# A place for each head pair's O in chunk 0, and all of Q of chunk 6 projected in chunk 5

## What is computed

```python
Q, K, V = split_heads(x @ WQ.T), split_heads(x @ WK.T), split_heads(x @ WV.T)   # 16 heads of 64
scores = where(causal, Q @ K.T / sqrt(64), NEG)
out = (softmax(scores) @ V) @ WO.T
x = layernorm(x + out)                                   # x: [16, 2048, 1024]
xn = x * rsqrt(mean(x * x) + 1e-6)
scale = 127.0 / max(abs(xn))                             # per row
xq = clip(round(xn * scale), -128, 127) / scale
x = layernorm(x + xq @ (w_int8 * weight_scale).T + bias)
```

## Time and profile before

| | us |
|---|---|
| runs of the kernel (median of 3) | 1003.89 (1002.97 to 1004.13) |
| the profiled execution | 1004.11 |
| its span on the slowest core (core 2) | 1002.6 |
| spans of the eight cores | 994.9 to 1002.6 |
| TensorE busy | 907.1 (90%) |
| ScalarE busy | 687.2 (69%) |
| VectorE busy | 519.0 (52%) |
| GpSimd busy | 227.4 (23%) |

### The profile page before, as it was taken

How to read it: one execution, slowest core, us unless ns; L and a number is a source line. 1 busy time by engine, 2 the same in 40 slices (tenths; PEclk the granted TensorE clock), 3 DMA queues, 4 the chain that set the end, 5 groups by cost and what they waited for, 6 DMA issues and landing times.

```text
span 1002.6 us, 22536 instructions; the slowest of 8 cores (994.9 to 1002.6 us)
## 1 busy us (share of the span) xinstructions
PE 907.1 (90%) x8267; PEld 409.9 (41%) x8416; DVE 519.0 (52%) x1263; ACT 687.2 (69%) x713; POOL 227.4 (23%) x290
## 2 busy tenths in 40 slices
PE   3894999999999989999999999999799999999863
PEld 1342444444444433434444444444344444444421
DVE  0110147744786327653127747762477523776675
ACT  0133666776877789999744566777577779999931
POOL 5021322231122121221223232232122211222101
PEclk9997999999999999999999999999899999999897
DMA  9999333250223141221154251144413210114212
GB/s 117 146 178 182 65 45 42 64 147 13 28 64 101 54 53 28 79 44 62 37 66 66 64 148 23 33 107 94 49 33 102 74 44 10 25 26 146 62 56 63
DMA packets 99289, 71.18 MB, mean 71 GB/s; under 512 B 70384, under 2 KB 88816, under 8 KB 99184
## 3 DMA queue, kind: packets, MB, share of 16 engines
q1 hardware_dynamic: 78368, 50.87, 20.5%
q0 software_dynamic: 20816, 18.88, 14.8%
HBM read 55.05 MB, written 16.78 MB: 72 GB/s over the span
## 4 chain that ended last, share of the span: by engine, by line
PE 77%; DMA 8%; ACT 6%; issue 3%; DVE 3%; POOL 1%; DVEq 0%; POOLq 0%; ACTq 0%; SPq 0%
PE ps L324 47%; PE ps L640 16%; PE ps L531 14%; ACT PT L559 5%; DMA WV<-wvt 4%; DMA QO<-OS 2%; DMA XT<-xt 1%; DVE OS L682 1%; DMA QT<-QB 1%; POOL PT L574 1%; ACT Q L844 1%; POOL WK L148 0%; POOL WQ L148 0%; DVE SM L678 0%; DVE Z L749 0%
## 5 line engine op out<-in xcount | busy, mean ns | idle before, releaser
L559 ACT ACTIVATE PT<-ps,SM 128x1024 bf16<-128x1024 f32 (+2 forms) x576 | 586.2, 1066 | 151.8 <-PE ps L531 149.8
L574 POOL TENSOR_TENSOR PT<-PT,MASK 128x256 bf16<-128x256 bf16 (+1 forms) x184 | 158.2, 867 | 506.0 <-ACT PT L559 505.8
L640 PE MATMUL ps<-VX,PT 128*128 128x65 bf16 x4352 | 235.1, 195 | 25.4 <-DVE OS L682 22.6
L640 PEld LDWEIGHTS ps<-VX,PT 128*128 128x128 bf16 x4352 | 179.2, 98 | 177.0 <-issue 141.9
L531 PE MATMUL ps<-QO,KT 64*128 64x512 bf16 (+1 forms) x1504 | 193.3, 325 | 10.9 <-ACT PT L559 10.2
L324 PE MATMUL ps<-XT,WK 128*128 128x512 bf16 x486 | 126.0, 386 | 23.8 <-DMA XT<-xt 22.4
L324 PE MATMUL ps<-W,QT 128*128 128x512 bf16 x477 | 128.6, 385 | 17.5 <-DMA QT<-QB 13.8
L324 PE MATMUL ps<-WO,QO 128*128 128x512 bf16 x474 | 127.0, 378 | 4.2 <-issue 1.7
L324 PE MATMUL ps<-XT,WQ 128*128 128x512 bf16 x485 | 124.6, 380 | 2.5 <-DMA WQ<-wqt 1.1
L324 PE MATMUL ps<-WV,XT 128*128 128x512 bf16 x489 | 124.1, 383 | 2.7 <-DMA WV<-wvt 1.4
L531 PEld LDWEIGHTS ps<-QO,KT 64*128 64x128 bf16 x1504 | 51.7, 94 | 182.2 <-issue 177.3
(11 more groups left out here) (50 smaller groups left out, 546.5 us busy)
## 6 DMA issues: line engine op xcount, KB each, us to landing
Z<-x SPq DMA_DIRECT2D x32, 512.0 KB, 4.4
y<-Z SPq DMA_DIRECT2D x32, 512.0 KB, 2.8
XT<-xt POOLq DMA_DIRECT2D x7, 1024.0 KB, 12.5
WK<-wkt POOLq DMA_DIRECT2D x4, 512.0 KB, 21.4
WQ<-wqt POOLq DMA_DIRECT2D x4, 512.0 KB, 24.6
WV<-wvt POOLq DMA_DIRECT2D x2, 1024.0 KB, 42.2
WO<-wot POOLq DMA_DIRECT2D x1, 2048.0 KB, 70.6
W<-w8t POOLq DMA_DIRECT2D x1, 2048.0 KB, 87.1
```

The costliest lines, as they stand in the source:

```text
L559: emit("s", lambda eng: eng.activation(dst, src, AF.Exp, bias=EB, scale=0.125).then_inc(sem["s"], 1))
L574: emit("g", lambda eng: eng.tensor_tensor(blk, blk, msk, ALU.mult).then_inc(sem["m"], 1))
L640: last = eng.matmul(ps[:, o_at + s_ * o_head + q * 65: o_at + s_ * o_head + q * 65 + 65], PT[:, pt0 + s_ * 512 + c0: pt0 + s_ * 512 + c0 + ...
```

## The change

There are two parts. In chunk 0 (su = 0) each head pair's normalized O has a place of its own: the pairs 0 and 1 in OS, the pairs 2 and 3 in O6, a bf16 view of the memory of Q16, and the pairs 4 to 7 in QT8. With that VectorE waits for no transpose in chunk 0, and each pair's transpose has a semaphore of its own. From chunk 1 on all is as before. And chunk 5 is treated like chunk 2: the four late projections of Q of chunk 6 stand at the end of the fillers of chunk 5 instead of at the head of those of chunk 6.

```diff
+        O6 = at("O6", [128, 1024], BF16, "q16")
...
+        for j in range(8):
             sem["ot%d" % j] = e(nc.semaphore("sem_ot%d" % j))
...
             wait("v", t_tok())
-            if i >= 2:
+            if su:
                 wait("v", tok_ot[(i - 2) // 8, (i - 2) % 8])
-            o0 = (i % 2) * 512
+            out, o_row, o0 = OS, 1024, (i % 2) * 512
+            if su == 0 and i >= 2:
+                out, o_row, o0 = ((O6, 1024, (i - 2) * 512) if i < 4 else
+                                  (QT8, 2048, (i - 4) * 512))
...
-                    ap(OS, o0, (1024, 128), (64, 2), (128, nq), (1, 64)),
+                    ap(out, o0, (o_row, 128), (64, 2), (128, nq), (1, 64)),
...
-            key = "ot%d" % (i % 2)
+            key = "ot%d" % (i % 2 if i >= 8 else i)
...
-                OS[:, o0:o0 + nq * 128]).then_inc(sem[key], 16))
+                out[:, o0:o0 + nq * 128]).then_inc(sem[key], 16))
...
-                if g == 2:
+                if g in (2, 5):
                     order, late = order + late, []
```

## The result

The change makes the kernel slower by 0.4%: the ratio of the time after to the time before is 1.0039 (95%: 1.0024 to 1.0054). Four runs of the changed kernel take 1005.97 to 1009.09 us, against a median of 1003.65 before; its other four (1052 to 1134 us) and one of the eight before are of a slower kind that some runs of either kernel fall into, and they are left out. The forecast was 1000.9 us, with a range to 1004.5: wrong in sign, and the result lies outside the range.

The account below looks back on a forecast made before the run. TensorE was taken to bound the kernel. Core 2: 1002.6-15.5+9.4+0.5+0.5 = 997.5 us; core 6: 1001.9-12.4+9.4+1.0+0.5 = 1000.4. With time outside the span, 1000.9 us was taken, nearer core 6; range 996.5 to 1004.5.

Parts of the forecast that it names:

- Part one, in each of its steps: Chunk 0: VectorE's wait on transposes and TensorE's clock drop go, saving 15.5 us on core 2, 12.4 on core 6.
- no new wait at the first WO: Start of chunk 1: piled-up transposes delay the first WO projection by 0 to some 5 us; 0 taken.
- The mechanism of the longer stall in chunk 6: Chunk 6: TensorE reaches K of chunk 7 before XT's load is issued, so the stall grows by 9.4 us.
- both times that lead to it: Chunk 6, after scores begin: TensorE reaches K of chunk 7 at about 3.3 us; the load is issued at 4.75.
- Its clock drop: After chunk 6's stall: a clock drop on every core, costing 0.5 us more on core 2, 1.0 on core 6.
- so they cost in one what they save in the other … I take 0.5: Chunks 5 and 6: the four moved projections, 6.9 us of TensorE, nearly cancel; bound 0 to 6.9, 0.5 us taken.
- half of the 6.9 us moved is not given back: Rival: chunk 6 becomes ScalarE's and returns only half the moved work; 1003.9 us, no change; chance 0.09.
- The last sign that the prediction named for being wrong: Chunk 5 grows by 6.9 us and chunk 6 without its stall does not shrink by as much.
- a landing of 13.0 us that does not change: Chunk 6: XT's load for chunk 7 lands 13.0 us after issue on core 2, 12.8 on core 6, as before.
- the rival of the shorter load: Chunk 6: XT's load lands in 10.3 us on the slow cores, stall 2.7 us less; 998.2 us; chance 0.16.
- taken to stay below core 6: Whole kernel: the six cores other than 2 and 6, shorter now, stay below core 6's forecast span of 1000.4 us.
- The estimate of 6.8 us from the Trainium skill: Chunk 6's XT load: 2.0 us plus bytes at 436 GB/s; stall 8.2 us, kernel near 995; trace preferred.

Follow-up runs that it names:

- e1_part1: Kernel before with only the change's new places for O in chunk 0, chunks 5 and 6 as before: 989.04 us, ratio 0.9880.
- e6_hold_debt: Changed kernel with chunk 7's projections counted ready only 13 us after their load is put out, and chunk 7's old filler order: 988.61 us, ratio 0.9879.
- e5_p1_hold: Kernel before with part one, and chunk 7's projections counted ready only 13 us after their load is put out; no part two: 983.09 us, ratio 0.9823.
- e4_hold: Changed kernel with chunk 7's projections counted ready only 13 us (planner's clock) after their load is put out: 991.87 us, ratio 0.9915.
- e9: Changed kernel with chunk 7's old filler order and nearly all exps of chunk 6 cut to one head of a pair: 997.57 us.
- e10: Part one with chunk 7's projections held until their load is due, and nearly all exps of chunk 6 cut to one head of a pair: 979.45 us.
- e2_part2: Kernel before with only the four projections of Q of chunk 6 moved into chunk 5, chunk 0 as before: 1020.22 us, ratio 1.0192.
- e3_debt: Changed kernel with the planner's fill debt at the start of chunk 7 set as before, restoring that chunk's filler order: 1001.16 us, ratio 1.0005.
- e8_order7: Part one with chunk 7's projections held until their load is due, plus the changed kernel's filler order in chunk 7: 987.40 us, ratio 0.9867.
- e7_after: The changed kernel, unaltered, run again beside the experiments against the kernel before: 1005.74 us, ratio 1.0051.

## Why the prediction was wrong

**Right.** Part one, in each of its steps: 40.4 us from the first to the eighth pair, no clock drop near 90 us, no new wait at the first WO, which starts 8.5 us behind the eighth pair's reciprocal (forecast 121-112.5). e1_part1 shows it alone. The mechanism of the longer stall in chunk 6 was also right, and both times that lead to it to within 0.3 us (3.45 against 3.3, 4.48 against 4.75): where the landing time did not change, on the cores 4 and 5, the stall grew by 9.1 us of the 9.4 forecast. Its clock drop came on every core, 10.2 to 17.1 us of half clock from 685 to 693 us on, where before two had none. But most of that lies in the stall itself, where it costs nothing; after the stall TensorE runs at half clock for 2.6 to 5.1 us, 3.7 in the mean against 3.2 before, and on core 2 for 3.8 instead of 5.3.

**Wrong: "so they cost in one what they save in the other … I take 0.5".** This is the first step that failed. Chunk 5 was charged 6.5 us, and the rest of chunk 6 gave back 1.6, so the term was 4.9 us. The bound of 0 to 6.9 held the truth, and the value taken did not; e6_hold_debt against e5_p1_hold prices the move at 5.5. The reason given, that ScalarE is only 77% busy in chunk 6, is one for an average. In single steps TensorE did wait: in the rest of chunk 6 longer for exps and normalizations than before (3.3 us instead of 1.8), and in its head at the very first scores (e4_hold, e6_hold_debt), where the moved projections had stood. TensorE idled 2.9 of 90 us there already, which was a sign, while chunk 5 with 0.95 idle in 98 us pays for all that is added. The rival "half of the 6.9 us moved is not given back" (chance 0.09) came nearest, though it had only ScalarE as the reason, and e9 and e10 put less than half of what is missing in the rest of chunk 6 down to it. The last sign that the prediction named for being wrong, chunk 5 growing and chunk 6 without its stall not shrinking by as much, is the one that came.

**Wrong by omission: chunk 7.** No term of the sum is for it, and it costs 3.9 us. I compared the orders at the two places that the change names. The planner is one pass over the whole program, and a debt of 9.5 ns in place of 86.7 changed the order two chunks on. That the order differed there could be read before any run. That it would cost 3.9 us could not be worked out as easily, but "other order in chunk 7" is a rival with its own price, and with it the range would have had to reach past 1006.

**Wrong in size: the stall.** The sum has +9.4 us, and 0.5 to 1.0 for the clock, from a landing of 13.0 us that does not change. Landing fell to 9.2 on core 2, and the stall grew by 5.3 us there. On the cores 4 and 5, whose landing stayed the same, it grew by 9.1, near the full 9.4. So this term was too high for core 2 (the rival of the shorter load had it), and the other cores, "taken to stay below core 6", came up to the slow ones: spans were 994.9 to 1002.6 and are 999.9 to 1007.6. In the mean the stall grew by 7.5 us and the head of chunk 6 by 7.2, although some 10 matmuls (2 us) had left it. The quickest landing of the eight cores is 8.6 us. The estimate of 6.8 us from the Trainium skill (DMA: Bandwidth & Descriptors, Anatomy of one DMA) stays under all of them.

**In sum.** By the stages' means the prediction has -13.7 right (to the tenth by luck: chunk 0 took 54.1 us in the profile before and 53.1 in e2_part2), some +10 where 7.2 came, 0.5 where 6.5-1.6 = 4.9 came, and 0 where 3.9 came. The last two turn the sign: 8.8 us against 0.5. With chunk 7's order restored (e3_debt) the kernel is even with the one before, 1001.16 against 1000.70, so the forecast's gain of 3 us was not there even without chunk 7's loss.

## What to carry to other kernels

Work that is moved from one stage to another was paid in full where TensorE had no idle time, and refunded only in part where it had some; read both stages' idle time, and what the moved work had been covering, before calling a move neutral, and price each stage by itself. Where one planner pass lays out the whole program, compare the order of the whole program and not only the edited place: a difference of 77 ns in a carried debt moved fillers two chunks later and cost 4 us. And a piece of work is better counted as ready when its data will have landed, not when its load is issued: that one condition (e4_hold, e5_p1_hold) took 14 us off the changed kernel and 6 off the one with part one alone.

## What the runs showed of the hardware

- A short wait at a tight place can cost more than itself, but not each time. With the changed order of chunk 7 one wait of 1.57 us stands in place of waits of at most 0.73, and a stretch at 1.2 GHz (granted clock 0.50) of 3.4 to 6.8 us begins in it or within 2 us of it on 35 of 40 cores, on all eight in the change and in e8_order7; with the order of before 8 of 56 cores have one near that place. On core 5 of the change TensorE had been busy 7.64, 7.12 and 7.35 of 8 us in the three stretches ahead of it; at the same distances in the kernel before it was busy 7.64, 7.55 and 6.84 and kept 2.4 GHz. In e7_after core 5 was busy 7.64, 7.12 and 7.34, had the same wait, and kept 2.4 GHz too, so neither the wait nor these sums decide it alone, and what does stays open. That the order makes the drop likely, e3_debt and e8_order7 show.
- The same load of XT, 2.1 MB read, landed in 8.4 to 13.0 us over cores and kernels. Before, it was issued at 706.55 us and a DMA transpose of SyncE followed 1.7 us later (708.24); in the changed kernel the transpose went first (its issue ends at 689.34, the load's begins at 690.20) and landing was 1.7 us shorter in the mean. The other profiles fall in the same two groups: 9.5 to 10.4 us in the mean of the cores with part two (six more), 10.5 to 11.3 without it (four more). That the transpose is the cause was not tried.
